# Attention scores on one core: operand rows copied by way of DRAM, row maxima carried as two fp32 halves, scores by key issued ahead of the wait for the maxima

## Chip, core and metric

One core of a Trainium2 chip runs the whole program. The metric is device time in microseconds of one execution. The kernel is written in raw instructions for five engines (TensorE, VectorE, ScalarE, GpSimd and SyncE; PE, DVE, ACT, POOL and SP in the rows), each with its own queue, and tied together with semaphores.

## What is computed

Four layers, each a cross attention and a feed-forward net, on 4096 tokens of 128 numbers (x) with a context of the same size. Three of the four attentions are the same kind and concern us: 16 heads of width 8, 32 tiles of 128 queries. The reference for them, cut to what matters:

```python
# L0: projections with biases
score = jnp.einsum('bhij,bhjk->bhik', qh, kt) / math.sqrt(d)      # d = 8
attn = jax.nn.softmax(score, axis=-1)
out = jnp.einsum('bhls,bhsd->bhld', attn, vh)
# L2: one set of keys and values shared by all 16 heads
attn_score = jnp.einsum('bhid,bjd->bhij', qh, k) / np.sqrt(D_HEAD)
# L3: as L0, with a mask by key and a causal mask
m = mask[:, None, :, None] + future[None, None, :, :]
scores = jnp.where(m != 0, NEG, scores)
```

A softmax needs the maximum of each row of scores. The kernel computes it exactly and takes it off before the exponential.

## The kernel before, in words

**Stages.** By the profile's clock the program runs: L0's attention (about 50 to 235 us), the feed-forward net, attention and net of the next layer (to 485), L2's attention (485 to 708), its net of eight experts (to 825), L3's attention (825 to 1090), and the last net (to 1162).

**A half.** An attention walks over 32 tiles, and each tile in two halves of 8 heads: 64 halves in an attention, 192 in all. The order on each engine is written out by hand, in `pair_of_scores(u, g, v, f)` and the functions around it. For one half TensorE does:

- *scores by key* for tile u into banks 2 and 3: keys on the partitions, 4 heads x 128 queries along a row. L1402 in L0, L1353 in L2 (one moving operand of 512 columns for each of two row groups), L1359 in L3 (8 instructions of 128 columns). They wait for t_ex, ScalarE having emptied banks 2 and 3.
- *scores by query* for tile v = u + 2 into banks 0 and 1, only to find the row maxima: L1405 in L0, L1362 in L2 and L3 (8 instructions of 128 columns). They wait for t_mx, VectorE having taken the maxima out of these banks (L1867), and for operands_in, the DMAs of their rows.
- In L3 both get a mask by further small bf16 matmuls ahead (L1390 by key, L1395 by query, 8 each).
- *the maxima*: L1416 adds minus the row maximum to banks 2 and 3, waiting for t_nm.
- ScalarE's exponential of the two banks (L1046, 128x1024), and on TensorE the weighted values of the half before (L1434, 8 instructions in two passes, 16 records).

The array's 128 rows are used as four groups of 32. The keys' scores of a half lie on two groups and the queries' scores on the other two, so instructions of both can run side by side. The maxima's matmul uses 12 rows of the same two groups as the keys' scores. The weighted values use all 128 rows.

**How a maximum reaches the banks.** VectorE reduces (L1867) to negative maxima, 16 numbers a query. They are split into three bf16 parts by four small operations: on GpSimd in L0 and L3 (`split_maxima`, L802 to L808), on VectorE in L2 (L1924, L1926, L1934, L1946). TensorE transposes the parts (L1485), and VectorE multiplies the transposed rows with 0/1 columns into `nmax_one` (L1904, 128x512 bf16), which L1416 sums over with ones as the stationary operand.

**Operand rows.** In L2 and L3 the projections are made per quad of four tiles (L1551, L1555, L1561), copied out by ScalarE (L1068 into `q_all`, L1078 into `k_all`), split by VectorE into upper bits and rest (L1875, L1878; t_half counts them). Then SP's `rows_of_quad` spreads them from SBUF to SBUF over the row groups (L599): 64 KB a DMA, 20 DMAs a quad in L2 (4 of k, 16 of q) and 32 in L3 (16 and 16). ScalarE may write `k_all` and `q_all` of the next quad only once all row DMAs of the quad before have landed (`staging_free`).

## Time and profile before

| | before |
|---|---|
| time, median of 3 runs | 1161.0 us (1151.83 to 1170.66) |
| the profiled execution | 1163.81 us, its span 1162.1 us |
| mean granted TensorE clock | 0.818 of full speed |
| busy: PE, DVE, ACT, POOL | 954.1, 772.6, 621.9, 471.6 us |
| chain that ended last | PE 59%, DVE 21%, issue 10%, ACT 3%, SP's queue 3% |

The page is one execution. "Busy" is the time an engine worked on instructions; "granted clock" is TensorE's clock in tenths or parts of full speed, which has the levels 1.0 (2.4 GHz) and 0.5 (1.2 GHz), so a mean of 0.75 over a stretch says that half of it was at each level. The chain is the sequence of work that ended last, and "issue" in it is time in which the engine waited for nothing that the profile shows.

### The profile page before, as it was taken

The numbers are of one execution on the slowest core, as the hardware profiler recorded it, in microseconds if no ns is written. First come the engines' busy times: TensorE is split into PE (matmuls) and PEld (weight loads), VectorE is DVE, ScalarE is ACT, GpSimd is POOL, SyncE is SP. The second block draws the span as 40 slices with busy tenths as digits, with TensorE's granted clock in tenths as the row PEclk, the third lists the DMA queues.
The fourth block names the chain that finished last, engine by engine and source line by source line (L and its number), as shares of the span: only waits on it lengthen the run. The fifth ranks groups of instructions, "written<-read, shape, count | busy, mean of one in ns | idle before, by whom it ended". The sixth has DMA issues, their size and how long they took to land.

```text
span 1162.1 us, 30498 instructions
## 1 busy us (share of the span) xinstructions
PE 954.1 (82%) x10213; PEld 661.9 (57%) x10213; DVE 772.6 (66%) x2053; ACT 621.9 (54%) x1387; POOL 471.6 (41%) x999
## 2 busy tenths in 40 slices
PE   3889898967777556789988899888698888899999
PEld 3644444424455233356666666787555556566798
DVE  3567877758978798488777764374258667765344
ACT  3556666547756566266455434455434455433366
POOL 5421467632145243102333445677411377773100
PEclk9999999975678687698667758999868888865699
DMA  6979676457799930222122205768442233330011
GB/s 181 157 82 90 63 99 81 69 114 173 95 177 181 176 54 1 56 75 54 51 56 55 56 11 158 200 170 262 118 117 74 75 93 110 111 92 2 3 34 36
DMA packets 326321, 112.33 MB, mean 97 GB/s; under 512 B 224873, under 2 KB 299657, under 8 KB 326186
## 3 DMA queue, kind: packets, MB, share of 16 engines
q1 hardware_dynamic: 319834, 94.40, 43.7%
q0 software_dynamic: 5488, 15.88, 4.4%
q8 instruction: 82, 1.34, 0.5%
q14 instruction: 53, 0.43, 0.1%
q10 hardware_dynamic: 864, 0.27, 0.1%
HBM read 50.70 MB, written 35.51 MB: 74 GB/s over the span
## 4 chain that ended last, share of the span: by engine, by line
PE 59%; DVE 21%; issue 10%; ACT 3%; SPq 3%; POOL 2%; DMA 2%; another core or an unknown queue 0%; DVEq 0%; ACTq 0%; POOLq 0%
PE bank L1434 8%; DVE nmax L1867 7%; PE bank L1402 5%; PE bank L1524 4%; PE bank L1416 3%; PE bank L1765 3%; PE bank L1719 3%; PE bank L1359 3%; PE bank L1731 3%; PE bank L1773 2%; SPq L599 2%; PE bank L1533 2%; PE bank L1362 2%; PE bank L1281 2%; PE bank L1561 2%
## 5 line engine op out<-in xcount | busy, mean ns | idle before, releaser
L1867 DVE TENSOR_REDUCE nmax<-bank 128x8 f32<-128x1024 f32 x192 | 234.5, 1221 | 126.6 <-PE bank L1362 83.9
L1046 ACT ACTIVATE probs_space<-bank 128x1024 f32<-128x1024 f32 x192 | 196.7, 1024 | 190.1 <-PE bank L1416 188.7
L1434 PE MATMUL bank<-probs_space,vals 128*32 128x128 f32 x3072 | 149.4, 322 | 3.0 <-issue 3.0
L1434 PEld LDWEIGHTS bank<-probs_space,vals 128*32 128x32 f32 x3072 | 84.9, 124 | 77.7 <-issue 70.5
L1362 PE MATMUL bank<-k_rows,q_rows 32*128 32x128 f32 x1024 | 106.7, 337 | 6.8 <-DMA q_rows<-q_all 6.8
L1362 PEld LDWEIGHTS bank<-k_rows,q_rows 32*128 32x128 f32 x1024 | 88.9, 241 | 10.0 <-DMA q_rows<-q_all 7.7
L802 POOL CAST nmax_parts<-nmax 128x16 bf16<-128x16 f32 x64 | 12.6, 198 | 198.8 <-DVE nmax L1867 184.7
L1416 PE MATMUL bank<-nmax_one,ones_bf 12*128 12x512 bf16 x384 | 91.0, 452 | 0.0
L727 POOL TENSOR_TENSOR var_b<-stats 128x8 f32<-128x8 f32 (+3 forms) x33 | 7.4, 225 | 203.3 <-DVE stats L1802 201.8
L1402 PE MATMUL bank<-q_one,k_all 32*128 32x512 f32 x256 | 72.9, 636 | 19.8 <-DVE nmax L1867 16.7
L1904 DVE TENSOR_TENSOR nmax_one<-bank,max_row 128x512 bf16<-128x512 bf16 x96 | 65.6, 684 | 20.2 <-PE bank L1485 17.0
L1405 PE MATMUL bank<-k_one,q_all 32*128 32x512 f32 x256 | 73.0, 643 | 1.7 <-DVE nmax L1867 0.9
L1802 DVE BATCH_NORM_STATS2 stats<-x 128x6 f32<-128x128 f32 x230 | 61.2, 287 | 5.0 <-DMA x<-in_x_dram 2.0
L960 POOL DMA_INDIRECT token_rows<-early,slot_row_int x46 | 48.6, 1057 | 30.0 <-DVE early L2245 21.2
L1931 DVE RECIPROCAL o_inv<-bank 128x16 f32<-128x16 f32 x96 | 24.4, 254 | 53.7 <-PE bank L1533 53.7
L786 POOL TENSOR_TENSOR late<-bf_up,late 128x512 f32<-128x512 f32 x36 | 56.7, 1598 | 0.1
L734 POOL TENSOR_TENSOR var_a<-var_b,minus_half 128x8 f32<-128x8 f32 (+3 forms) x33 | 53.9, 1633 | 2.6
L1731 PE MATMUL bank<-moe_w,probs_space 128*128 x368 | 50.4, 281 | 4.3 <-ACT probs_space L1241 2.3
L1353 PE MATMUL bank<-q_rows,k_rows 32*128 32x512 f32 x128 | 39.9, 614 | 16.7 <-DVE nmax L1867 15.5
L1359 PE MATMUL bank<-q_rows,k_rows 32*128 32x128 f32 x512 | 52.5, 331 | 0.0
L1731 PEld LDWEIGHTS bank<-moe_w,probs_space 128*128 128x128 f32 x368 | 46.0, 196 | 5.0 <-issue 5.0
L1266 ACT ACTIVATE q_one<-bank,up_bias 128x128 f32<-128x128 f32 x128 | 36.6, 369 | 20.4 <-PE bank L1765 20.4
(300 smaller groups left out, 2533.9 us busy)
## 6 DMA issues: line engine op xcount, KB each, us to landing
expert_rows<-zeros SPq DMA_DIRECT2D x8, 2322.0 KB, 34.6
q_rows<-q_all SPq DMA_DIRECT2D x256, 64.0 KB
k_rows<-k_all SPq DMA_DIRECT2D x160, 64.0 KB
context<-expert_w SPq DMA_DIRECT2D x31, 322.0 KB
k_one<-expert_w SPq DMA_DIRECT2D x15, 322.0 KB
late<-_L_ffn_down_weights_dram POOLq DMA_DIRECT2D x9, 512.0 KB, 5.6
late<-in_L_ffn_up_weights_dram POOLq DMA_DIRECT2D x9, 512.0 KB, 4.4
q_one<-expert_rows SPq DMA_DIRECT2D x46, 64.5 KB
```

The costliest lines, as they stand in the source:

```text
L786: pool.tensor_tensor(tmp(i), half(src, i % 2), weight, ALU.mult).then_inc(S("bf_step"), 1)
L1046: act.activation(probs[:, 2 * g:2 * g + 2, :, :].rearrange("k g i q -> k (g i q)"), bank_pair[1][:, :, :].rearrange("k g f -> k (g f)"), A ...
L1359: pe.matmul(bank[2 + s][:, at], operand(k_rows, u, 2 * g + s, i), operand(q_rows, u, 2 * g + s, i), start=not masked and i == 0, stop=False)
L1362: m = pe.matmul(bank[s][:, at], operand(q_rows, v, 2 * f + s, i), operand(k_rows, v, 2 * f + s, 0 if shared_keys else i), start=not masked ...
L1402: pe.matmul(bank[2 + s], group(k_all, u, 2 * g + s), group(q_one, u, 2 * g + s), start=True, stop=False)
L1405: m = pe.matmul(bank[s], group(q_all, v, 2 * f + s), group(k_one, v, 2 * f + s), start=True, stop=True)
L1416: m = pe.matmul(bank[2 + s], ones_bf[first:last, :], nmax_one[first:last, u % 2, :, :], start=False, stop=True)
L1434: m = pe.matmul(bank[4][32 * j:32 * j + 32, g * P:(g + 1) * P], v[:, first:first + VW], probs[:, 2 * g + j // 2, j % 2 * 2 + s, :], start= ...
L1731: m = pe.matmul(bank[(4, 6)[(t - 1) % 2]][:, 0:P], slot_hid[:, (t - 1) % 2, c * P:(c + 1) * P], w2[:, bass.ds(expert[t - 1] * HID + c * P, ...
L1802: dve.bn_stats(stats[:, u, :], x[:, u * P:(u + 1) * P]).then_inc(S("stats"), 1)
L1867: dve.tensor_reduce(nmax[:, u % 2, 0, :].rearrange("q (g i) -> q g i", i=HG)[:, 2 * g:2 * g + 2, :], bank_pair[0][:, :, :].rearrange("q g ...
L1904: dve.tensor_tensor(nmax_one[:, (t + 1) % 2, :, :], over_blocks(bank[6][:, 3 * P:4 * P].bitcast(BF16)[:, 0:P], HG), max_row[:, :].unsqueez ...
```

## The change

1. `NPART` is 2: a maximum is split into its upper bits and the rest, both fp32, by two small operations on VectorE in all three attentions (`halves_of_maxima`). GpSimd only waits for t_mx in its place.
2. VectorE's `nmax_one` goes. ScalarE copies the transposed 128x128 block to `nmax_rows` instead. The transposition is fp32.
3. The maxima's matmul: 8 instructions a half, each with a 0/1 column `max_row[rows, i]` broadcast over 128 columns as the stationary operand (8 rows) and 128 columns of `nmax_rows` moving, instead of 2 instructions of 12 rows and 512 columns.
4. The scores by key of a half, with their masks, are issued ahead of the waits for operands_in and t_mx and ahead of all scores by query. Before they were interleaved with them in L0 and L3.
5. Operand rows of q in L2, of q and k in L3: one DMA of the whole 512 KB tile to DRAM, a wait for it, and 4 DMAs of 256 KB back, one for each row group. 9 DMAs a quad in L2, 10 in L3. The first of a tile waits for both of its halves.

The core of the diff:

```diff
+            def rows_by_way_of_dram(halves, scratch, rows, of_row, out_name, n_out, name):
+                sp.dma_start(scratch[:, :, :], halves[:, :, :]).then_inc(S(out_name), 16)
+                sp.wait_ge(S(out_name), 16 * n_out)
+                for n in range(4):
+                    sp.dma_start(rows[n:P:4, :, :].bitcast(F32),
+                                 scratch[:, of_row[n], :].rearrange("(i r) f -> r i f", i=HG)).then_inc(S(name), 16)
...
                 def iteration(t):
+                    if live(t + 1):
+                        act.wait_ge(S("t_mt"), tiles + t + 2)
+                        past(act, "t_s2", 2 * (tiles + t))
+                        act.activation(nmax_rows[:, (t + 1) % 2, :], bank[6][:, 3 * P:4 * P], ACT.Copy
+                                       ).then_inc(S("t_nm"), 1)
...
                 def pair_of_scores(u, g, v, f):
                     if live(u):
+                        scores_by_key(u, g)
                     if live(v):
+                        scores_by_query(v, f)
...
                     if live(u):
                         pe.wait_ge(S("t_nm"), tiles + u + 1)
-                        for s in range(2):
-                            first = HR * (2 * g + s)
-                            last = first + NPART * HG
-                            m = pe.matmul(bank[2 + s], ones_bf[first:last, :], nmax_one[first:last, u % 2, :, :],
-                                          start=False, stop=True)
+                        for i in range(HG):
+                            for s in range(2):
+                                rows = slice(HR * (2 * g + s), HR * (2 * g + s) + NPART * HG)
+                                m = pe.matmul(bank[2 + s][:, i * P:(i + 1) * P],
+                                              max_row[rows, i:i + 1].broadcast_to([NPART * HG, P]),
+                                              nmax_rows[rows, u % 2, :], start=False, stop=i == HG - 1)
...
-                        dve.tensor_tensor(nmax_one[:, (t + 1) % 2, :, :], over_blocks(bank[6][:, 3 * P:4 * P].bitcast(BF16)[:, 0:P], HG),
-                                          max_row[:, :].unsqueeze(2).broadcast_to([P, HG, P]), ALU.mult
-                                          ).then_inc(S("t_nm"), 1)
...
+                        dve.tensor_scalar(upper.bitcast(I32), whole.bitcast(I32), UPPER_BITS, None, ALU.bitwise_and
+                                          ).then_inc(S("t_na"), 1)
...
+                        dve.tensor_tensor(rest, whole, upper, ALU.subtract).then_inc(S("t_na"), 1)
```

**TensorE in L2, one half, before.** L1353 are the scores by key, L1362 those by query, L1416 the maxima, L1434 the weighted values:

```order
L1485 MATMUL bank<-ident_bf,nmax_parts 128x128 [waits t_on,t_res,t_nm,t_na]
L1353 MATMUL bank<-q_rows_51,k_rows_55 128x512 [waits t_mx,operands_in1,t_ex]
L1353 MATMUL bank<-q_rows_51,k_rows_55 128x512
L1362 MATMUL bank<-k_rows_53,q_rows_49 128x128 x8
L1416 MATMUL bank<-nmax_one,ones_bf 128x512 [waits t_nm]
L1416 MATMUL bank<-nmax_one,ones_bf 128x512
L1434 MATMUL bank<-probs_space,vals 32x128 [waits t_ve,t_ue,t_ex]
```

The same place of the changed kernel (L1379 by key, L1398 by query, L1419 the maxima, L1438 the weighted values):

```order
L1489 MATMUL bank<-ident,nmax_halves 128x128 [waits t_on,t_res,t_nm,t_na]
L1379 MATMUL bank<-q_rows_51,k_rows_55 128x512 [waits t_ex]
L1379 MATMUL bank<-q_rows_51,k_rows_55 128x512
L1398 MATMUL bank<-k_rows_55,q_rows_51 128x128 [waits t_mx,operands_in0]
L1398 MATMUL bank<-k_rows_55,q_rows_51 128x128 x7
L1419 MATMUL bank<-nmax_rows,max_row 128x128 [waits t_nm]
L1419 MATMUL bank<-nmax_rows,max_row 128x128 x7
L1438 MATMUL bank<-probs_space,vals 32x128 [waits t_ve,t_ue,t_ex]
```

The waits for the maxima and for the rows moved from the first score by key to the first by query, and the maxima's matmul became eight instructions.

**TensorE in L3, one half, before** (L1390 and L1395 the masks by key and by query, L1359 and L1362 the scores by key and by query; a pair of each kind stands for eight):

```order
L1390 MATMUL bank<-quant_bf,future_rep 128x4x32 [waits t_mx,operands_in0,t_ex]
L1395 MATMUL bank<-ident_blocks_bf,past_rep 128x4x32
...
L1359 MATMUL bank<-q_rows_52,k_rows_56 128x128
L1362 MATMUL bank<-k_rows_53,q_rows_49 128x128
...
L1416 MATMUL bank<-nmax_one,ones_bf 128x512 [waits t_nm]
L1416 MATMUL bank<-nmax_one,ones_bf 128x512
L1434 MATMUL bank<-probs_space,vals 32x128 [waits t_ex]
```

The same place of the changed kernel (L1353 and L1376 mask and scores by key, L1362 and L1398 mask and scores by query):

```order
L1353 MATMUL bank<-ffn_wT,future_rep 128x4x32 [waits t_ex]
L1353 MATMUL bank<-ffn_wT,future_rep 128x4x32 x7
L1376 MATMUL bank<-q_rows_50,k_rows_54 128x128 x8
L1362 MATMUL bank<-ident_blocks_bf,past_rep 128x4x32 [waits t_mx,operands_in1]
L1362 MATMUL bank<-ident_blocks_bf,past_rep 128x4x32 x7
L1398 MATMUL bank<-k_rows_54,q_rows_50 128x128 x8
L1419 MATMUL bank<-nmax_rows,max_row 128x128 [waits t_nm]
L1438 MATMUL bank<-probs_space,vals 32x128 [waits t_ex]
```

Before, neighbours in the queue lie on different row groups and belong to different banks; now 16 instructions on two row groups stand ahead of 16 on the other two.

**SP in L3, the rows of a quad, before:**

```order
L599 DMA k_rows_53<-k_all 32x512 [waits t_half,t_s2]
L599 DMA k_rows_53<-k_all 32x512 x7
L599 DMA k_rows_53<-k_all 32x512 [waits t_half]
L599 DMA k_rows_53<-k_all 32x512 x7
L599 DMA q_rows_49<-q_all 32x512 [waits t_half]
L599 DMA q_rows_49<-q_all 32x512 x7
```

And changed:

```order
L606 DMA k_halves<-k_all 128x1024 [waits t_half,t_s2]
L609 DMA k_rows_53<-k_halves 32x4x512 [waits k_out]
L609 DMA k_rows_53<-k_halves 32x4x512 x3
L606 DMA q_halves<-q_all 128x1024 [waits t_half]
L609 DMA q_rows_49<-q_halves 32x4x512 [waits q_out]
L609 DMA q_rows_49<-q_halves 32x4x512 x3
```

Far fewer issues, and two waits for a DMA's completion that stand in SP's queue.

## Rows read from the trace of the kernel before

**Rows 1.** Windows: start:end, length, PE, PEld, DVE, ACT, POOL busy, clock, DMA.
```profile
75.00:225.00 150.00, 133.09 (x1574) 68.10 (x1570) 112.23 (x191) 98.32 (x160) 79.06 (x181) 0.99 0.71 83
490.00:705.00 215.00, 194.87 (x2160) 136.56 (x2158) 166.72 (x462) 108.86 (x200) 63.34 (x164) 0.71 0.19 49
845.00:1085.00 240.00, 212.60 (x3473) 144.70 (x3470) 155.44 (x275) 107.80 (x178) 115.52 (x225) 0.75 0.28 79
500.00:525.00 25.00, 20.74 (x327) 14.29 (x326) 22.36 (x50) 16.95 (x29) 0.00 (x0) 1.00 0.27 72
1050.00:1075.00 25.00, 25.00 (x342) 16.82 (x338) 13.44 (x23) 9.79 (x15) 8.92 (x23) 0.50 0.01 2
```

**Rows 2.** Timeline, L2 at full clock: start, duration, engine, line, output<-input, idle before.
```profile
512.17 0.68 DVE L1904 TENSOR_TENSOR nmax_one<-bank,max_row 128x512 bf16<-128x512 bf16 x1
512.40 0.50 PE L1353 MATMUL bank<-q_rows,k_rows 32*128 32x512 f32 x2 [1.15 <-DVE nmax L1867]
512.71 0.42 PE L1416 MATMUL bank<-nmax_one,ones_bf 12*128 12x512 bf16 x2
512.79 0.27 PE L1362 MATMUL bank<-k_rows,q_rows 32*128 32x128 f32 x2
513.06 0.64 PE L1434 MATMUL bank<-probs_space,vals 128*32 128x128 f32 x16
515.19 0.50 PE L1353 MATMUL bank<-q_rows,k_rows 32*128 32x512 f32 x2 [0.85 <-DVE nmax L1867]
```

**Rows 3.** Timeline, L2 at half clock, TensorE, same columns.
```profile
562.19 0.79 PE L1353 MATMUL bank<-q_rows,k_rows 32*128 32x512 f32 x2
562.79 0.65 PE L1416 MATMUL bank<-nmax_one,ones_bf 12*128 12x512 bf16 x2
562.90 0.41 PE L1362 MATMUL bank<-k_rows,q_rows 32*128 32x128 f32 x2
563.36 1.08 PE L1434 MATMUL bank<-probs_space,vals 128*32 128x128 f32 x16
565.10 0.79 PE L1353 MATMUL bank<-q_rows,k_rows 32*128 32x512 f32 x2
```

**Rows 4.** Timeline, L3 at full clock, TensorE.
```profile
907.80 0.21 PE L1390 MATMUL bank<-quant_bf,future_rep 32*128 32x128 bf16 x1 [1.04 <-DVE nmax L1867]
907.99 0.30 PE L1359 MATMUL bank<-q_rows,k_rows 32*128 32x128 f32 x1
908.47 0.41 PE L1416 MATMUL bank<-nmax_one,ones_bf 12*128 12x512 bf16 x2
```

**Rows 5.** Timeline, L3 at half clock, TensorE.
```profile
1056.22 0.28 PE L1390 MATMUL bank<-l_T,future_rep 32*128 32x128 bf16 x1
1056.58 0.45 PE L1359 MATMUL bank<-q_rows,k_rows 32*128 32x128 f32 x1
1057.48 0.65 PE L1416 MATMUL bank<-nmax_one,ones_bf 12*128 12x512 bf16 x2
```

**Rows 6.** One maxima part on VectorE: least/median/most ns, first and last start.
```profile
L1926 DVE TENSOR_TENSOR nmax<-nmax,nmax_parts x32: 174/175/309, 487.2 to 688.9; 128x16 f32<-128x16 f32 x32
```

**Rows 7.** ScalarE's copy of a transposed 128x128 block, same columns.
```profile
L1105 ACT ACTIVATE oT<-bank x96: 271/283/296, 91.1 to 1089.4; 128x128 f32<-128x128 f32 x96
```

**Rows 8.** Waits, 860 to 1090 us (L3): waiting instruction <- releaser: total, times, longest.
```profile
ACT k_all L1078 <- DMA q_rows<-q_all: 15.8, 5, 4.3
PE bank L1390 <- issue: 11.1, 5, 3.4
```

**Rows 9.** Timeline of SP's queue, ahead of L3.
```profile
818.25 10.94 SPq L599 DMA_DIRECT2D k_rows<-k_all  x16
829.23 10.17 SPq L599 DMA_DIRECT2D q_rows<-q_all  x16
```

**Rows 10.** DMA issues: count, KB each, median us from issue to landing.
```profile
x<-in_x_dram SPq DMA_DIRECT2D x2, 512.0 KB, 11.2
context<-token_rows SPq DMA_DIRECT2D x2, 512.0 KB, 5.0
```

More of the change, by code:

```diff
@@ L18 @@
 NG, HG = 4, 4
-NPART = 3
+NPART = 2
 HR = 32
@@ L214, in gated_layers, with halves_of_maxima @@
         ROW_BUFFERS = {"L2": (2, 0, 1), "L3": (0, 1, 3)}
+        def halves_of_maxima(v):
+            halves = nmax_halves[:, v % 2, :].rearrange("q (g n i) -> q g n i", g=NG, i=HG)
+            return nmax[:, v % 2, :].rearrange("q (g i) -> q g i", i=HG), halves[:, :, 0, :], halves[:, :, 1, :]
         def rows_of(buffers, layer, c):
@@ new lines, in mask_of_maxima @@
+                def mask_of_maxima(f):
+                    for b in range(HG):
+                        at = slice(HR * b, HR * b + HR)
+                        for s in range(2):
+                            rows = slice(HR * (2 * f + s), HR * (2 * f + s) + HR)
+                            pe.matmul(bank[s].rearrange("q (i k) -> q i k", i=HG)[:, :, at],
+                                      past_rep[rows, b, :], over_blocks(ident_blocks_bf[rows, :], HG),
+                                      start=b == 0, stop=False)
@@ new lines, in scores_by_key @@
+                def scores_by_key(u, g):
+                    if not own:
+                        pe.wait_ge(S("t_q23"), 2 * (u // QT + 1))
+                        pe.wait_ge(S("t_q01"), 2 * (u // QT + 1))
+                    past(pe, "t_ex", 2 * (tiles + u) + g)
+                    if masked:
+                        mask(u, g)
+                    for i in range(1 if layer != "L3" else HG):
+                        for s in range(2):
+                            if layer == "L3":
+                                pe.matmul(bank[2 + s][:, i * P:(i + 1) * P], operand(k_rows, u, 2 * g + s, i),
+                                          operand(q_rows, u, 2 * g + s, i), start=False, stop=False)
+                            elif own:
+                                pe.matmul(bank[2 + s], operand(k_rows, u, 2 * g + s, 0),
+                                          operand(q_rows, u, 2 * g + s, slice(0, HG)), start=True, stop=False)
+                            else:
+                                pe.matmul(bank[2 + s], group(k_all, u, 2 * g + s), group(q_one, u, 2 * g + s),
+                                          start=True, stop=False)
```

172 lines of the change are left out of this document (58 added, 114 removed).

## Prediction

> **What bounds the kernel now.** I read first the windows of the three attention stages, since the change touches nothing else. In L0, TensorE works 133.1 of 150 us at almost full clock, VectorE 112.2. In L2 it works 194.9 of 215 us at a mean clock of 0.71, in L3 212.6 of 240 us at 0.75 [rows 1]. A mean of 0.71 is 42% of the time at full clock and 58% at half, 0.75 is half and half. So the engine that sets the end changes with the clock, and I read one half of a tile at each level.
>
> L2 at full clock: from one first score to the next is 2.79 us (512.40 to 515.19), and before both TensorE had stood idle, for 1.15 and 0.85 us, until VectorE had the maxima [rows 2]. VectorE is busy 22.4 of 25 us there, TensorE 20.7 [rows 1]: VectorE is the bound, with 2.5 us of work a half. L2 at half clock: 2.91 us a half and no idle time before the next one [rows 3]; TensorE is the bound. L3 late in the stage: half clock, TensorE busy 25.0 of 25 us [rows 1]. L3 at full clock waits for VectorE as L2 does, 1.04 us in the half shown [rows 4]. Beside that L3 has a loss of its own: ScalarE's copy into k_all waits 15.8 us for the last row DMAs of the quad before, in 5 places, and TensorE's next mask loses 11.1 us behind it in 5 places [rows 8]. SP's queue needs 10.9 us for the 16 row DMAs of k of one quad and 10.2 for q's, which stand behind them [rows 9].
>
> **Maxima's matmul.** Now its start is 0.35 us ahead of the weighted values at full clock (512.71 to 513.06) and 0.57 us at half (562.79 to 563.36) [rows 2, 3]. It becomes four rounds of 128 columns on two row groups, in a 4-byte type. Four rounds of scores of that size take 0.48 us at full clock (907.99 to 908.47) and 0.90 us at half (1056.58 to 1057.48) [rows 4, 5]. If the rounds were all, the price would be 0.48 − 0.35 = 0.13 and 0.90 − 0.57 = 0.33 us a half; if a tail of some 0.13 us follows the last round, as it seems to do now, 0.26 and 0.46. I take 0.22 and 0.41. The second pass of the transposition lies within these bounds.
>
> **VectorE.** It loses the 0.68 us product once a tile [rows 2], 0.34 us a half. In L2 it also does two small operations instead of four, of 0.175 us each [rows 6]: another 0.17 us a half. In L0 and L3 it gains two of them, so its net relief is 0.17 us a half. GpSimd's relief is worth nothing, for its parts are ready a tile ahead. ScalarE takes on 0.28 us a tile [rows 7] and is busy 16.95 of 25 us in L2's full-clock stretch [rows 1], so it has the room. While its copy waits for the transposition, the next exponential is queued behind it, and that one needs the maxima anyway.
>
> **L0.** TensorE is the bound: 64 halves x 0.22 = +14 us. Its idle time is 16.9 of 150 us [rows 1], mostly waits for VectorE, 0.2 to 0.3 us a half; VectorE's relief of 0.17 takes back 11 of it. Sum +3 us, bounds −5 (all idle time gone by the early scores by key) and +14.
>
> **L2.** At full clock VectorE falls from 2.5 to 2.0 us a half and TensorE is late next, with 20.74/25 x 2.79 = 2.31, plus 0.22: 2.53, say 2.6 us instead of 2.79. At half clock TensorE gets 0.41 us longer. The 215 us are some 32 halves at full (90 us) and 32 at half clock (125 us, 3.9 us each with projections and routing). With the same share of clocks: 32 x −0.2 + 32 x 0.41 = +6 us. But the clock is half in stretches that follow idle time on TensorE (it is full through L0, where the idle share is 11%, and through the first 25 us shown of L2), and that idle time goes: 17% idle at full clock becomes some 3%. I assume that half of the slow halves turn fast: 48 x 2.6 + 16 x 4.3 = 194, −21 us. If all did, 64 x 2.6 = 166, −49 us.
>
> **L3.** Two waits go. The stall behind the row DMAs: a 512 KB write and four reads of 256 KB. Nearest rows: 5.0 us for 512 KB from DRAM, 11.2 us where the queues are crowded [rows 10]. Write and reads (together 512 KB again) take 10 us for k and as much for q, 20 us in all, against 21.1 now [rows 9], 45 if crowded. I read the 10 us as a bound from above, since the four reads are in flight beside each other and the queues are not crowded in L3 (DMA share 0.28 [rows 1]). I take 7 us each: the 11 us of issue [rows 8] go. The waits for the maxima are 27.4 idle us of 240 [rows 1] less these 11, so 16; the scores by key now run within them, and VectorE is faster. Against that 31 halves x 0.22 and 33 x 0.41 = +20. Sum with the same clocks: −11 − 16 + 20 = −7 us. With half of the slow halves turned fast, at 0.8 us each, −20 us. Bounds −35 and +5. This holds if scores by key and by query still lie beside each other, which is the first rival's point.
>
> **Stage starts.** L3's first 32 row DMAs take 21 us in SP's queue (818.25 to 839.4) [rows 9] with TensorE idle. With 7 to 10 us for k and as much for q the way by DRAM takes 14 to 20 us: −5 us, bounds −7 and 0; if the writes took the crowded 11.2 us, +11.
>
> The Trainium skill (DMA: Bandwidth & Descriptors, Anatomy of one DMA) puts a fixed cost of about 2 us on each DMA, most of it the receipt for the write. Two DMAs in a row, for k and then for q, would pay it four times, an estimate of 8 us; the stall and the start would still shorten, and no row here parts the fixed cost from the rest.
>
> **Sum.** +3 − 21 − 20 − 5 = −43 us. Against the profiled execution's 1163.8 us that is 1121; the execution lies 2.8 us above the median of 1161.0, so I forecast 1119 us.
>
> **Rival 1, slower: keys and queries one after the other.** In L3 16 instructions on two row groups now stand ahead of the 16 on the other two. Before they alternated, and four groups worked together: masks and scores of both took 0.67 us (907.80 to 908.47) or 1.26 us at half clock [rows 4, 5]. If TensorE starts no instruction ahead of an earlier one, the same work takes twice that. At half clock that is 1.26 us x 33 halves = +42 us. At full clock the waits cover 0.4 of 0.67: +9 us. The gain of the covered waits and of the clock goes with it: L3 = −11 + 20 + 51 = +60 us, in all 3 − 21 + 60 − 5 = +37, so 1200 us. For it speaks the order alone. Against it: a maxima's matmul at 512.71 starts before the last pair of scores by query at 512.79, which stands ahead of it in the queue and lies on other groups, and so at 562.79 and 562.90 [rows 2, 3]. So a later instruction passes an earlier one, at least over two. Over 16 nothing shows. It decides where the depth is under some 8 instructions. I give it 0.27.
>
> By the Trainium skill (TensorE: Matmul & The Clock Gate, Step-by-step) only weight loads are pulled ahead and matmuls stay in program order, which is this rival, 1200 us. The two pairs of rows named just now disagree with the strict form of it. The same passage gives the queue that looks ahead a depth of 64, within which these 32 instructions with their loads would fit if matmuls did pass.
>
> **Rival 2, no change: the clock stays as it is.** The longer maxima's matmul is paid where TensorE is the bound, and the shares of the clock don't move: +3 + 6 − 7 − 5 = −3, 1158 us. For it speaks that late L3 is at half clock while TensorE is busy all the time [rows 1], so a full queue alone doesn't bring the clock back. Chance 0.22.
>
> **The numbers.** The forecast has 0.51, with its own range of 1075 to 1145 (L2 −49, L3 −35 at one end, the smaller halves of each at the other). A measurement tells about 2% from no change, 23 us: faster is below 1138. Forecast's case: 0.46 faster, 0.05 same. Rival 2: 0.03 faster, 0.18 same, 0.01 slower. Rival 1: 0.01 same or faster, 0.26 slower. Faster 0.49, same 0.24, slower 0.27. The range of 1075 to 1205 leaves out less than 0.2.
>
> **What the changed profile would show.** The line L1419 about 0.5 us ahead of L1438 at full clock. In L2 VectorE's busy share falling from 89% to 75 or 80% at full clock, and TensorE's wait for L1867's successor mostly gone; a mean clock above 0.8 in L2 if the assumption on it is right, near 0.71 if rival 2 is. In L3 the first mask by query within 0.1 us of the first mask by key where both are released (rival 1: 0.6 us or more behind). No "issue" wait of several us at the masks, and k_all's copy without its wait. SP: 10 DMAs a quad within 15 us. I would be wrong most of all by the depth over which TensorE passes instructions, then by the clock.

## Result, and the profile after

The changed kernel takes 1139.0 us (median of 20 executions, 1121.2 to 1161.6) beside 1167.3 us of the kernel before (median of 20), 28.3 us or 2.4% less. Ratios with an interval, here and in the table of experiments, compare only the quicker executions of each kernel, those within some 1.5% of its quickest: 0.971, with a 95% interval of 0.967 to 0.974. The forecast was 1119 us against 1161.0, a ratio of 0.964. The numbers below are those of one profiled execution each (before 1163.8 us, after 1140.5 us).

The windows of the three attentions L0, L2 and L3, from the start of the first to the start of the last exponential of each: start:end, length, busy time of PE, PEld, DVE, ACT and POOL, granted clock, DMA share, GB/s.

```profile
64.30:256.60 192.30, 178.46 (x2242) 122.67 (x2243) 122.44 (x246) 119.27 (x215) 69.93 (x104) 0.96 0.63 73
507.50:700.40 192.90, 183.79 (x2470) 139.37 (x2472) 134.02 (x352) 110.85 (x228) 61.93 (x159) 0.80 0.22 72
852.80:1062.60 209.80, 201.14 (x3741) 157.36 (x3745) 150.08 (x297) 107.39 (x203) 89.73 (x97) 0.85 0.36 118
```

The same stretches of the kernel before, read in the same way from its trace, were 178.9, 204.5 and 225.7 us, at a clock of 0.99, 0.73 and 0.76. So L0 lost 13.4 us, L2 gained 11.6, L3 gained 15.9, and the stretch between L2 and L3 went from 157.5 to 152.4 us, −5.1. The rest of the span gave 4.1 us, together 23.3 (1162.1 to 1138.8). In all three attentions TensorE is now busy 93 to 96% of the time; its idle time fell from 19.7 to 9.1 us in L2 and from 27.4 to 8.7 us in L3.

Two of the costliest groups of the page. The first answers to VectorE's maxima of before (L1867), the second to the maxima's matmul L1416 (384 instructions, now 1536). VectorE's product (0.68 us each in [rows 2]) has no line any more.

```profile
L1872 DVE TENSOR_REDUCE nmax<-bank 128x8 f32<-128x1024 f32 x192 | 234.2, 1220 | 155.7 <-PE bank L1398 94.4
L1419 PE MATMUL bank<-nmax_rows,max_row 8*128 8x128 f32 x1536 | 154.0, 321 | 0.0
```

**How keys and queries lie beside each other.** TensorE's timeline in L3 at full clock, to be laid beside [rows 4]. L1353 and L1376 are mask and scores by key, L1362 and L1398 mask and scores by query, L1419 the maxima.

```profile
881.79 0.40 PE L1353 MATMUL bank<-quant_bf,future_rep 32*128 32x128 bf16 x8
881.99 0.30 PE L1376 MATMUL bank<-q_rows,k_rows 32*128 32x128 f32 x2
882.03 0.28 PE L1362 MATMUL bank<-ident_blocks_bf,past_rep 32*128 32x128 bf16 x4
882.14 0.27 PE L1376 MATMUL bank<-q_rows,k_rows 32*128 32x128 f32 x2
...
882.25 0.38 PE L1376 MATMUL bank<-q_rows,k_rows 32*128 32x128 f32 x4
...
882.47 0.27 PE L1419 MATMUL bank<-nmax_rows,max_row 8*128 8x128 f32 x2
882.49 0.27 PE L1398 MATMUL bank<-k_rows,q_rows 32*128 32x128 f32 x2
...
883.01 0.64 PE L1438 MATMUL bank<-probs_space,vals 128*32 128x128 f32 x16
```

The first mask by query starts at 882.03, when six of the eight scores by key that stand ahead of it in the queue have not started (882.14 and 882.25). It starts 0.24 us behind the first mask by key, neither at the same time nor behind all 16. The maxima then start at 882.47, ahead of the last scores by query. From the first mask to the weighted values is 1.22 us (881.79 to 883.01). Before it was 0.67 us to the maxima [rows 4] and 0.34 from there, 1.01.

At half clock, beside [rows 5]:

```profile
1039.96 0.61 PE L1353 MATMUL bank<-l_T,future_rep 32*128 32x128 bf16 x8
1040.33 0.46 PE L1376 MATMUL bank<-q_rows,k_rows 32*128 32x128 f32 x2
1040.37 0.50 PE L1362 MATMUL bank<-ident_blocks_bf,past_rep 32*128 32x128 bf16 x6
1040.58 0.42 PE L1376 MATMUL bank<-q_rows,k_rows 32*128 32x128 f32 x2
...
1041.22 0.42 PE L1419 MATMUL bank<-nmax_rows,max_row 8*128 8x128 f32 x2
...
1042.21 1.08 PE L1438 MATMUL bank<-probs_space,vals 128*32 128x128 f32 x16
```

2.25 us from the first mask to the weighted values, 1.26 + 0.58 = 1.84 before. 0.41 us more, which is the price of the maxima that the forecast took.

**L2 at full clock**, beside [rows 2]:

```profile
543.03 0.50 PE L1379 MATMUL bank<-q_rows,k_rows 32*128 32x512 f32 x2
543.13 0.44 PE L1398 MATMUL bank<-k_rows,q_rows 32*128 32x128 f32 x4
...
543.37 0.23 PE L1419 MATMUL bank<-nmax_rows,max_row 8*128 8x128 f32 x2
...
543.85 0.64 PE L1438 MATMUL bank<-probs_space,vals 128*32 128x128 f32 x16
...
545.19 0.50 PE L1379 MATMUL bank<-q_rows,k_rows 32*128 32x512 f32 x2
```

2.16 us a half (543.03 to 545.19) where it was 2.79, and these two halves start without the idle time of 1.15 and 0.85 us of before. Over the whole of L2 TensorE's wait for the maxima fell from 15.5 to 1.3 us, and it now waits 6.3 us for ScalarE's exponential at the scores by key. From the maxima to the weighted values 0.48 us instead of 0.35. VectorE's busy share at full clock is 87% in one stretch of 25 us (520 to 545) and 77% in another (507.5 to 535); it was 89%.

**SP's queue in L3**, the quickest quad, beside [rows 9]:

```profile
891.37 0.33 SPq L606 DMA_DIRECT2D k_halves<-k_all  x1
893.95 2.67 SPq L609 DMA_DIRECT2D k_rows<-k_halves  x4
897.15 0.33 SPq L606 DMA_DIRECT2D q_halves<-q_all  x1
901.50 2.53 SPq L609 DMA_DIRECT2D q_rows<-q_halves  x4
```

From the issue of a write of 512 KB to the first read behind it, which waits for the write, it is 2.58 and 4.35 us here, and all issues end 12.7 us after the first. Later in L3 the write of q takes up to 7.7 us (975.80 to 983.54), and the quads take 12.7 to 18.0 us. Before, the 32 issues of a quad took 21.1 us ahead of L3 and 21.6 to 23.8 us in it.

### The profile page after: what moved, and what is told of

Read it like the earlier page. It is cut to its first block, busy times and chain, and to the rows that moved or that the text cites. A ratio compares the mean times of both kernels' runs of the same rounds, so it can differ in the third digit from the quotient of the medians.

```text
span 1138.8 us, 32253 instructions
## 1 busy us (share of the span) xinstructions
PE 971.3 (85%) x11365; PEld 732.8 (64%) x11365; DVE 743.7 (65%) x2022; ACT 635.7 (56%) x1483; POOL 418.0 (37%) x743
## 4 chain that ended last, share of the span: by engine, by line
PE 57%; DVE 20%; issue 8%; ACT 6%; DMA 3%; POOL 3%; SPq 1%; another core or an unknown queue 0%; ACTq 0%; DVEq 0%; POOLq 0%
PE bank L1438 7%; PE bank L1419 5%; PE bank L1382 5%; DVE nmax L1872 5%; ACT probs_space L1042 4%; PE bank L1528 3%; PE bank L1398 3%; PE bank L1777 2%; PE bank L1769 2%; PE bank L1723 2%; PE bank L1735 2%; PE bank L1537 2%; PE bank L1379 2%; DVE small L2041 2%; DVE stats L1806 2%
## 5 line engine op out<-in xcount | busy, mean ns | idle before, releaser
L1419 PE MATMUL bank<-nmax_rows,max_row 8*128 8x128 f32 x1536 | 154.0, 321 | 0.0
L1419 PEld LDWEIGHTS bank<-nmax_rows,max_row 8*128 8x128 f32 x1536 | 128.8, 211 | 22.4 <-issue 18.1
L1438 PE MATMUL bank<-probs_space,vals 128*32 128x128 f32 x3072 | 141.7, 309 | 0.7 <-issue 0.7
L1398 PE MATMUL bank<-k_rows,q_rows 32*128 32x128 f32 x1024 | 96.5, 311 | 7.0 <-DMA q_rows<-q_halves 4.9
L1438 PEld LDWEIGHTS bank<-probs_space,vals 128*32 128x32 f32 x3072 | 81.2, 119 | 20.1 <-issue 4.2
L1398 PEld LDWEIGHTS bank<-k_rows,q_rows 32*128 32x128 f32 x1024 | 80.1, 216 | 11.8 <-issue 6.0
L1382 PE MATMUL bank<-q_one,k_all 32*128 32x512 f32 x256 | 75.7, 664 | 13.8 <-ACT probs_space L1042 13.4
L796 POOL TENSOR_TENSOR late<-bf_up,late 128x512 f32<-128x512 f32 x36 | 56.7, 1591 | 50.1 <-DVE nmax L1872 49.9
L956 POOL DMA_INDIRECT token_rows<-early,slot_row_int x46 | 48.6, 1057 | 35.0 <-DVE early L2232 26.2
L796 POOL TENSOR_TENSOR late<-bf_dn,late 128x256 f32<-128x256 f32 x36 | 31.3, 887 | 75.6 <-DVE nmax L1872 64.5
L1376 PE MATMUL bank<-q_rows,k_rows 32*128 32x128 f32 x512 | 45.9, 302 | 0.0
L941 POOL DMA_INDIRECT expert_rows<-late,dest_int x32 | 32.1, 1004 | 35.1 <-DVE dest_int L1963 28.1
```

The lines of the kernel that those rows point to most:

```text
L796: pool.tensor_tensor(tmp(i), half(src, i % 2), weight, ALU.mult).then_inc(S("bf_step"), 1)
L956: pool.indirect_dma_start(out=token_rows, out_offset=bass.IndirectOffsetOnAxis(ap=slot_row_int[:, s_no:s_no + 1], axis=0), in_=slot_y[:, s ...
L1382: pe.matmul(bank[2 + s], group(k_all, u, 2 * g + s), group(q_one, u, 2 * g + s), start=True, stop=False)
L1398: m = pe.matmul(bank[s][:, i * P:(i + 1) * P], operand(q_rows, v, 2 * f + s, i), operand(k_rows, v, 2 * f + s, 0 if layer == "L2" else i), ...
L1419: m = pe.matmul(bank[2 + s][:, i * P:(i + 1) * P], max_row[rows, i:i + 1].broadcast_to([NPART * HG, P]), nmax_rows[rows, u % 2, :], start= ...
L1438: m = pe.matmul(bank[4][32 * j:32 * j + 32, g * P:(g + 1) * P], v[:, first:first + VW], probs[:, 2 * g + j // 2, j % 2 * 2 + s, :], start= ...
```

## Experiments

The change has three parts that can stand alone: the maxima (M), the order (O) and the rows by way of DRAM (R). The kernels below have them one by one, in pairs and by layer. The theory was that of the forecast: each part pays or costs in its own place. The rival theory was that a part's worth depends on the others, since a wait taken away only shows the next one.

| kernel | parts | ratio to before | 95% | medians of all, us: this / before | L0, L2, L3: us from first to last exponential |
|---|---|---|---|---|---|
| before | | 1 | | | 178.9, 204.5, 225.7 |
| e3 | M | 1.013 | 1.004 to 1.022 | 1160.4 / 1153.2 | 193.7, 197.3, 225.3 |
| e8 | O | 1.006 | 1.001 to 1.011 | 1162.1 / 1162.5 | 179.1, 203.2, 226.2 |
| e7 | R | 0.975 | 0.968 to 0.981 | 1131.0 / 1162.5 | 179.0, 201.9, 201.9 |
| e6 | O, R | 0.970 | 0.962 to 0.977 | 1128.5 / 1162.5 | 176.2, 204.8, 201.6 |
| e1 | M, R | 0.997 | 0.990 to 1.004 | 1146.4 / 1153.2 | 208.9, 195.1, 225.3 |
| e2 | M, O | 1.004 | 0.998 to 1.011 | 1153.9 / 1153.2 | 193.1, 178.1, 230.0 |
| after | M, O, R | 0.971 | 0.967 to 0.974 | 1139.0 / 1167.3 | 192.2, 192.9, 209.7 |
| e5, the same again | M, O, R | 0.972 | 0.960 to 0.984 | 1139.0 / 1162.5 | 198.2, 198.0, 210.0 |
| e4 | O, R; M not in L0 | 0.966 | 0.955 to 0.977 | 1102.2 / 1153.2 | 178.4, 168.3, 209.9 |
| e9 | O, R; M in L2 alone | 0.959 | 0.949 to 0.969 | 1121.5 / 1165.2 | 178.3, 192.9, 199.2 |
| e10 | R; M in L2 alone | 0.970 | 0.964 to 0.977 | 1132.3 / 1165.2 | 183.6, 208.0, 200.1 |
| e11 | R in L3 alone | 0.975 | 0.969 to 0.981 | 1134.8 / 1165.2 | 178.9, 205.5, 200.4 |
| e12 | R, each tile written 3 times | 1.056 | 1.049 to 1.062 | 1230.3 / 1165.2 | 177.6, 217.5, 270.3 |

The last column is one execution each, and L2's length in it moves with the granted clock. In executions of one and the same kernel the time follows the clock too: of the changed kernel's 20, the one at a mean clock of 0.822 took 1161.6 us and one at 0.864 took 1121.2 us. e1's profile is the slowest of its executions, at 0.809. Each kernel is compared with executions of the kernel before on the same chip, which themselves have medians from 1153.2 to 1167.3 us. So the ratios decide, and the last column only where differences are large or come back in several kernels.

Read as a cube of three parts, the ratios say: R is worth 1.6 to 3.6% in all four of its pairs (before to e7, e8 to e6, e3 to e1, e2 to after). M costs 1.3% alone (e3) and 2.2% beside R (e7 to e1), and nothing clear of the noise beside O (e8 to e2, e6 to after). O gives 2.6% beside M and R (e1 to after); beside M (0.9%) and beside R (0.5%) the intervals overlap, and alone it is 0.6% slower.

**e1: order of before, maxima and rows as changed.** In `pair_of_scores`:

```diff
-                    if live(u):
-                        scores_by_key(u, g)
-                    if live(v):
-                        scores_by_query(v, f)
...
+                    if live(u):
...
+                        past(pe, "t_ex", 2 * (tiles + u) + g)
+                    if live(v):
+                        if own:
+                            name, landed = operands_in(layer, v // QT)
+                            pe.wait_ge(S(name), landed)
...
+                        past(pe, "t_mx", 2 * (tiles + v) + (1 - f))
...
+                    if own:
+                        scores_of_heads(u, g, v, f)
```

> The changed kernel with the matmuls' order and waits of before: the wait for the maxima and the rows stands ahead of the first score by key, and in L0 and L3 scores by key and by query alternate again. Theory A (the early scores by key fill waits for the maxima in L3 and L2): L3's attention, 209.7 us from first to last exponential, goes up by 8 to 16 us, L2's (192.9) by 2 to 5, L0's (192.2) stays; in all some 1152 us. Theory B (the early issue is worth nothing, and 16 instructions on two row groups ahead of the other 16 delay the scores by query by the 0.4 us that the trace shows at half clock): L3 goes down by 5 to 10 us, in all 1132 us.

Ratio 0.997 where the whole change has 0.971: taking the order back costs some 2.6%, about 30 us, more than twice what theory A had. Theory B falls. By stages L3 rose by 15.6 us and L2 by 2.2, as A had it, but L0 rose by 16.7 us too, where A had nothing; its clock was 0.88 beside 0.96. This one profile is of the slowest execution, so how the loss divides over the stages is not shown. In L3 TensorE again waits 11.9 us for the maxima, 4.0 in the changed kernel.

**e2: row DMAs of before, maxima and order as changed.**

```diff
-        N_ROW_DMAS = {"L2": 4 + 4, "L3": 4 + 4}
+        N_ROW_DMAS = {"L2": HG * (1 + HG), "L3": HG * (HG + HG)}
...
-                    rows_by_way_of_dram(k_all, k_halves, rows_of(k_rows, layer, c), K_HALVES, "k_out", c + 1, name)
+                                    sp.dma_start(rows_of(buffers, layer, c)[n:P:4, i, :].bitcast(F32),
+                                                 halves[HR * at:HR * at + HR, upper, :]).then_inc(S(name), 16)
```

> The changed kernel with the row DMAs of before (20 a quad in L2, 32 in L3, from SBUF to SBUF). Theory A (the way by DRAM took away ScalarE's stall ahead of k_all and shortened the idle stretch before L3): L3 goes up by about 11 us, the stretch from L2's last to L3's first exponential (152.4 us) by 5, in all 1155 us. Theory B (the stall was only the place where TensorE's slack showed): less than 3 us more in L3, in all 1144 us.

Ratio 1.004: without the rows nothing of the gain is left, 3.3% or nearly 40 us, more than theory A's 16 us. The two profiled executions are 18.7 us apart: L3 rose by 20.3 us (A had 11), the stretch ahead of it by 5.8, and L2 fell by 14.8 us at a clock of 0.88 beside 0.80. The waits in L3 (850 to 1080 us; waiting instruction, releaser, total, times, longest):

```profile
ACT k_all L1070 <- DMA q_rows<-q_all: 9.5, 4, 4.1
PE bank L1358 <- DMA q_rows<-q_all: 6.3, 3, 3.4
```

TensorE no longer stands before the masks for the maxima; it stands before those by query (L1358), for the rows. The early scores by key uncovered the late rows.

**e3: the maxima alone** (the changed kernel with the two edits of e1 and e2 together).

> The kernel of before with the new maxima alone (two fp32 halves on VectorE, ScalarE's copy, eight matmuls of 8 rows): old order, old row DMAs. Theory A (each part acts in its own stage): L0 up by 13 us as in the changed kernel (178.9 to 192), L2 down by 8 to 12 (204.5 to 194), L3 up or down by under 5: 1165 to 1170 us beside 1167 of before. Theory B (VectorE's relief is only worth something once the early scores by key are there): L2 stays at 204 us and the kernel is 10 to 20 us slower than before, 1180 us.

Ratio 1.013, and 1.006 by the medians. L0 at 193.7 us, +14.8, L2 at 197.3, −7, L3 the same: theory A nearly stage by stage. Its total, within 3 us of before, is missed: 7 us slower by the medians, 15 by the ratio, whose interval ends above 1. A half in L3 at half clock in the old order shows the price of the maxima's matmul alone:

```profile
1056.66 1.06 PE L1413 MATMUL bank<-nmax_rows,max_row 8*128 8x128 f32 x8
1057.65 1.08 PE L1432 MATMUL bank<-probs_space,vals 128*32 128x128 f32 x16
```

0.99 us from its start to the weighted values, 0.57 before in L2 [rows 3]: +0.42.

**e4: the maxima of before in L0 alone.**

```diff
+                            if layer == "L0":
+                                m = pe.matmul(bank[2 + s], ones_bf[first:first + 3 * HG, :],
+                                              nmax_one[first:first + 3 * HG, u % 2, :, :], start=False, stop=True)
...
+                    if live(t + 1) and layer == "L0":
+                        dve.tensor_tensor(nmax_one[:, (t + 1) % 2, :, :], over_blocks(bank[6][:, 3 * P:4 * P].bitcast(BF16)[:, 0:P], HG),
+                                          max_col[:, :].unsqueeze(2).broadcast_to([P, HG, P]), ALU.mult
+                                          ).then_inc(S("t_nm"), 1)
```

> The changed kernel, but L0 keeps the maxima of before (three bf16 parts by GpSimd, VectorE's product, two matmuls of 12 rows and 512 columns); L2 and L3 are as changed, order and rows too. Theory A (L0's +13 us is the longer maxima's matmul, 64 x 0.2 us, on an engine that has no slack there): L0 falls from 192 back to about 179 us, in all 1126 us, faster than both kernels. Theory B (L0 lost the time by the order, all scores by key ahead of the wait): L0 stays at 190 us or more, in all 1138 us.

L0 is back at 178.4 us with the new order in it: theory A. The order did not cost L0 its time; the maxima did. TensorE is busy 163.4 us in this L0 and 178.5 in the changed kernel's, a difference of 15.0 us, about that of the lengths (13.8). The edit puts back the split, the product and the matmul of two instructions at once, so it doesn't say which of them it is. The ratio of 0.966 is below the change's, though the intervals overlap.

**e5: the changed kernel once more**, on the same chip as e6 to e8.

> The changed kernel once more, on the same chip as the next three, as their measure. Both theories: 2 to 3.5% under the kernel of before (0.965 to 0.98).

0.972, as before.

**e6: order and rows without the new maxima.**

```diff
-NPART = 2
+NPART = 3
...
-                        for i in range(HG):
-                            for s in range(2):
-                                rows = slice(HR * (2 * g + s), HR * (2 * g + s) + NPART * HG)
...
+                        for s in range(2):
...
+                            m = pe.matmul(bank[2 + s], ones_bf[first:last, :], nmax_one[first:last, u % 2, :, :],
+                                          start=False, stop=True)
```

> The kernel of before with the new order and the way by DRAM, the maxima as before (the third part of the change left out). Theory A (each part pays in its own place, and the new maxima cost L0 13 us and give L2 some 10): L0 at 179 us from first to last exponential, L2 at 195 to 203, L3 at 205 to 212; 20 to 30 us faster than before, as fast as the whole change. Theory B (the early scores by key and the faster rows only pay once VectorE is relieved): L3 stays above 218 us and the kernel within 10 us of before.

0.970, L3 at 201.6 us: theory A, and more than it said in L3; L2, at 204.8, gained nothing. The whole change, with the new maxima, has 210 us in L3: there they cost 8 us.

**e7: the rows alone**, the kernel of before with the new `rows_of_quad`.

> The kernel of before with the way by DRAM alone. Theory A (the two losses seen in the trace of before go: 11 us of issue behind ScalarE's k_all, 5 us of start): 12 to 18 us faster than before, L3 at 212 to 216 us, no wait of k_all's copy for a DMA. Theory B (taking the rows away from the kernel with the early scores cost 29 us by the medians, so rows are worth most where the rest is fast): under 10 us faster here.

0.975. One part, nearly all of the whole change's gain. L3 falls from 225.7 to 201.9 us, 24 us where theory A had 10 to 14. One wait of k_all's copy for the rows is left, 3.8 us.

Where in L3 the time went is seen when the stage is cut in two: from the 1st to the 49th of its 64 exponentials (six quads), and from there to the last (two quads). The columns are those of the windows above. First the kernel before:

```profile
857.89:1026.92 169.03, 141.63 (x2626) 97.20 (x2629) 122.81 (x222) 82.07 (x140) 87.79 (x172) 0.85 0.34 95
1026.92:1083.60 56.68, 56.68 (x741) 39.32 (x745) 26.87 (x47) 21.19 (x33) 26.06 (x46) 0.50 0.10 28
```

e7:

```profile
849.10:1012.32 163.22, 138.78 (x2626) 96.16 (x2629) 126.93 (x222) 81.75 (x139) 88.19 (x172) 0.86 0.42 136
1012.32:1051.04 38.72, 35.55 (x741) 25.56 (x744) 26.23 (x47) 19.52 (x33) 26.39 (x46) 0.91 0.15 51
```

The changed kernel:

```profile
852.84:1005.39 152.55, 145.59 (x2916) 113.02 (x2917) 123.08 (x242) 85.58 (x163) 68.92 (x76) 0.93 0.46 148
1005.39:1062.57 57.18, 55.47 (x831) 44.28 (x830) 26.95 (x56) 21.78 (x40) 20.81 (x22) 0.64 0.11 38
```

And e6:

```profile
857.60:1021.09 163.49, 148.95 (x2629) 112.75 (x2632) 129.16 (x221) 81.56 (x139) 88.00 (x171) 0.84 0.41 136
1021.09:1059.19 38.10, 35.82 (x741) 27.46 (x738) 26.48 (x48) 19.51 (x33) 26.56 (x47) 0.91 0.14 48
```

Before and e7 do the same work. TensorE's idle time is the same too, 27.4 and 27.6 us. 5.8 of the 24 us were saved in the first 48 halves, where the stalls were, and 18.0 in the last 16, which took 56.7 us at half clock before and 38.7 at 0.91. Before, TensorE works 1.87 of the 4 us from 1022 to 1026, then the clock falls and stays at half to the end of the stage, though TensorE is busy without a gap. In e7 it falls at about 1013, is back at full at about 1019 and stays there. So most of the gain is the same instructions run faster at the end of the stage. What decides whether the clock comes back is not shown.

The other kernels repeat this within a few microseconds. With the new rows and the old maxima in L3 (e6, e7, e9, e10, e11) the last 16 take 38.1 to 38.7 us; in all others 53.6 us or more. With M, O and R in L3 (after, e5, e4) the two parts are 152.6 to 152.8 and 57.2 us. So the 8 us that the new maxima cost L3 beside O and R are a gain of 11 us in the first part and a loss of 19 in the second, where the changed kernel's clock falls for the last time at 1028 and does not rise again.

**e8: the order alone.**

> The kernel of before with the new order alone. Theory A (scores by key run in the wait for the maxima, 16 us in L3 and 15 us in L2): 8 to 15 us faster than before, TensorE's wait for VectorE's maxima under 6 us in L3. Theory B (the wait only moves: VectorE is the bound at full clock, the row DMAs come next): within 5 us of before, and TensorE waits for the row DMAs at the scores by query.

1.006, and 1.000 by the medians: no gain. Theory B, by these waits in L3 (850 to 1080 us):

```profile
ACT k_all L1078 <- DMA q_rows<-q_all: 22.0, 5, 6.8
PE bank L1361 <- DMA q_rows<-q_all: 15.6, 6, 5.1
PE bank L1361 <- DVE nmax L1869: 2.0, 4, 0.7
```

TensorE's wait for the maxima, 16.2 us before, is 2.0 us; 15.6 us of wait for the rows have come instead, and ScalarE's wait for them grew from 15.8 [rows 8] to 22.0.

**e9 and e10: new maxima in L2 alone, with the new and with the old order.** e9 is e4 with L3 treated as L0; e10 has e1's edit besides.

```diff
-                            if layer == "L0":
+                            if layer != "L2":
```

> The changed kernel with the new maxima in L2 alone: L0 and L3 keep three bf16 parts by GpSimd, VectorE's product and two matmuls of 12 rows and 512 columns; new order and rows everywhere. Theory A (the new maxima's matmul costs where TensorE is the bound, 0.2 us a half at full and 0.4 at half clock, and pays only in L2, where VectorE is): L0 177 to 180 us from first to last exponential, L2 168 to 195 by the clock granted, L3 200 to 203 instead of 210; a ratio of 0.945 to 0.96. Theory B (L3's 210 us with the new maxima beside 202 without were the difference of two executions): L3 stays at 208 or more and the ratio at 0.965.

> The same with the order and waits of before. Theory A (the early scores by key are worth nothing by themselves, as the order alone showed: 1.006): within 0.5% of the kernel above. Theory B (they pay where the row DMAs are fast and VectorE is relieved, as taking the order back from the whole change cost 1.4 to 2.5%): 10 to 20 us slower than the kernel above, most of it in L2.

e9 has the lowest ratio of all, 0.959: L0 178.3, L3 199.2, as theory A had it. Its interval ends at 0.969, below the change's estimate of 0.971 but not clear of its interval. By the medians of all executions e4 is ahead (0.956 beside 0.963), so which of the two is faster is not settled. e10 has 0.970; the order is worth 1% here, 11 us by the medians, and in the profiles 15 us in L2 (208.0 to 192.9) and 5 in L0. That is theory B of e10, with overlapping intervals. The order's worth beside the new maxima has the same sign in three pairs (e1 to after, e3 to e2, e10 to e9), and only the first is clear of the noise; without them it is no gain (before to e8) or half a percent within the noise (e7 to e6).

**e11: the way by DRAM in L3 alone.**

```diff
+                if layer == "L3":
+                    rows_by_way_of_dram(k_all, k_halves, rows_of(k_rows, layer, c), K_HALVES, "k_out", c + 1, name)
```

> The kernel of before with the way by DRAM in L3 alone (L2 keeps its 20 DMAs a quad). Theory A (ScalarE's stall was L3's: 32 issues a quad; L2's 20 fit): L3 at 202 us as with both, L2 at 202 to 205, ratio 0.975 to 0.98. Theory B: L2 gives a part too, and the ratio is 0.985 or more.

0.975, L3 at 200.4 and L2 at 205.5 us: the same as in both layers. With the old maxima L2's 20 DMAs a quad were in time anyway. With the new ones they are not quite: in L2 ScalarE's copy into k_all waits 7.9 us for them in e3 and 9.5 in e2.

**e12: each whole tile written three times.**

```diff
+                for again in (1, 2, 3):
+                    sp.dma_start(scratch[:, :, :], halves[:, :, :]).then_inc(S(out_name), 16)
+                    sp.wait_ge(S(out_name), 48 * (n_out - 1) + 16 * again)
```

> The kernel of before with the way by DRAM, each whole tile written to DRAM three times in a row, each time waited for, ahead of the four reads: some 6 us more for k and as much for q in a quad. Theory A (with 10 DMAs the rows have slack of over 10 us a quad, and being in time is all that they need): L3 at 202 to 206 us, only the stretch ahead of L3 longer by some 8 us; ratio 0.98. Theory B (every us in which the rows are later moves the work behind them): L3 at 212 to 226 us, k_all's copy waits for a DMA again, ratio 0.995 to 1.0.

1.056, much worse than theory B's 1.0. SP's queue for a quad:

```profile
908.04 7.18 SPq L604 DMA_DIRECT2D k_halves<-k_all  x3
917.50 2.53 SPq L607 DMA_DIRECT2D k_rows<-k_halves  x4
920.08 8.40 SPq L604 DMA_DIRECT2D q_halves<-q_all  x3
931.71 2.52 SPq L607 DMA_DIRECT2D q_rows<-q_halves  x4
```

and the waits in L3 (870 to 1150 us):

```profile
ACT k_all L1086 <- DMA q_rows<-q_halves: 52.4, 6, 10.4
PE bank L1398 <- issue: 47.0, 6, 9.7
```

The rows take 26.2 us from the first issue to the end of the last (908.04 to 934.23), 2 to 5 more than before, and L3 grows to 270.3 us, 45 more than before. ScalarE may write k_all only when q's last row of the quad before has landed, and ScalarE's next exponential is queued behind that copy. So a late row stops a ring of four engines, and the quads follow each other at the pace of the rows: 35.2 us from one to the next (908.04 to 943.22). With the old maxima L3 orders by the rows' issues a quad: 13 to 17 us give 199 to 202 us (e6, e7, e9, e10, e11), 21 to 24 give 226 (before, e8), 25 to 27 give 270 (e12). The new maxima break this order: e1 has 12 to 16 us a quad and an L3 of 225.3.

## Why the prediction was right or wrong

The direction came true, and the time lies within the forecast's own range of 1075 to 1145 us. The size is about half: −43 us were forecast, and the profiled executions are 23.3 us apart, the medians 28.3. L0 fell short by 10.4 us, L2 by 9.4, L3 by 4.1, and 4.1 us came from stretches that the sum left out. Two steps held, the price of the matmul and the start of L3. (The sum itself gives 1118, 1163.8 − 43 − 2.8; the 1119 is a slip of 1 us.) Of the signs, k_all's copy still waits 3.0 us for the rows in L3, and SP's 10 DMAs take 12.7 to 18.0 us a quad where 15 was the limit.

**Price of the maxima's matmul: right.** 0.22 and 0.41 us a half were taken; the traces show 0.13 us more from its start to the weighted values in L2 at full clock, 0.21 more in L3 from the first mask on, and 0.41 or 0.42 at half clock (after, e3).

**L0, +3: wrong, it was +13.4 (e3: +14.8, e5: +19).** The sum was 14 for the matmul less 11 for VectorE's relief. TensorE's busy time in L0 rose by 19.1 us (159.35 to 178.46), and its idle time fell by 5.7 (19.6 to 13.8). Two steps failed. The first is that L0 stays at full clock. Cut into eighths of 8 exponentials each, six of them are at full clock in the changed kernel and cost 4.4 us together, near the forecast. The third and the sixth are not, and cost 8.9. These two before:

```profile
107.29:131.68 24.39, 21.00 (x248) 11.13 (x248) 19.45 (x34) 15.32 (x26) 8.04 (x22) 1.00 0.63 48
178.56:201.36 22.80, 20.48 (x244) 10.65 (x244) 16.98 (x30) 15.26 (x26) 16.52 (x35) 1.00 0.79 94
```

and after:

```profile
110.38:136.95 26.57, 24.20 (x296) 16.86 (x296) 18.07 (x38) 15.98 (x31) 5.34 (x7) 0.94 0.56 44
185.82:215.36 29.54, 28.00 (x292) 18.33 (x292) 16.69 (x34) 16.22 (x30) 13.28 (x19) 0.77 0.60 72
```

L0 was at a clock of 0.88 to 0.96 in the kernels with the new maxima in it, and at 0.95 to 1.00 in the others. Why it falls there is not shown. The second failed step is "VectorE's relief of 0.17 takes back 11 of it". TensorE's wait for the maxima did vanish. In its place stands a wait of nearly the same length, in the changed kernel's L0 (64 to 257 us):

```profile
PE bank L1382 <- ACT probs_space L1042: 13.4, 22, 2.3
DVE nmax L1872 <- PE bank L1402: 55.5, 39, 3.2
```

The scores by key now wait for ScalarE's exponential in 22 places, as they waited for the maxima in 22 places before, 16.5 us then. The exponential is behind the maxima's matmul, so its added time is on this ring too; that is argued from the order, and no run parts it. VectorE has more idle time than before. e4 shows that it is the maxima: with the old ones L0 is at 178.4 us.

**L2, −21: half of it, −11.6.** The period at full clock fell further than forecast (2.16 us in the half shown, 2.6 taken). But the assumption that half of the slow halves turn fast came out at the clock going from 0.73 to 0.80, which is 54% of the time at half clock falling to 40%, a quarter of them. In five executions of kernels with new maxima and new order L2 took 168.3, 178.1, 192.9, 192.9 and 198.0 us at clocks of 0.92, 0.88, 0.80, 0.79 and 0.76. They differ in where the clock first falls: in e4 the first six eighths of L2 are at full clock (19.1 to 21.1 us each), in the changed kernel the first four. So the size of this term is the clock's, and one execution doesn't fix it; −6 to −36 us are all seen. Kernels with the old maxima had 202 to 206 us (before, e6, e7, e8, e11), those with the new ones and the old order 195.1, 197.3 and 208.0 (e1, e3, e10). So the new maxima shorten L2 in most executions, and more with the new order; that it needs both is not shown.

**L3, −20: near by its sum (−15.9), by luck, for its parts are wrong.** Forecast were −11 for the stall, −16 for the waits for the maxima, +20 for the matmul, and −13 for the clock. Measured: the rows alone give −24 (e7, e11), the new maxima cost 8 (e6 and e9 against after and e5), and the order gives nothing without them (e8: 226.2; e6 against e7: 201.6 and 201.9). The step that failed is to price the rows by the stall that the trace shows. Of their 24 us only 6 lie where the stalls were, and 18 in the last 16 halves, which before ran at half clock throughout.

**Stage start, −5: right, though not by the −5.1 above.** That stretch was 159.1 us with the new rows in e6 and 151.0 with the old ones in e3, so it doesn't measure the term. From the first row DMA to L3's first exponential it does: 39.6 and 39.4 us (before, e8) became 33.7 in e7 and e6, −6. k and q took 10.9 and 10.2 us of issues ahead of L3 [rows 9]; in the changed kernel the two writes with their waits and four reads each make some 13 us. The Trainium skill (DMA: Bandwidth & Descriptors, Anatomy of one DMA) has about 2 us of fixed cost a DMA, on the path of DMAs that GpSimd issues. The ones here are SyncE's; a write of 512 KB with its completion in 2.58 us leaves room for little more than that.

**Rival 1 (keys and queries one after the other, 1200 us): did not come.** The masks by query start when four to six of the scores by key ahead of them are still to start. The marker of the forecast, "within 0.1 us", was too strict: it is 0.24 us at full and 0.41 us at half clock. It costs nothing on the way to the weighted values: e6 has 1.04 us from the first mask to them at full clock, before it was 1.01:

```profile
1039.52 0.40 PE L1359 MATMUL bank<-l_T,future_rep 32*128 32x128 bf16 x8
...
1040.20 0.39 PE L1425 MATMUL bank<-nmax_one,ones_bf 12*128 12x512 bf16 x2
...
1040.56 0.64 PE L1443 MATMUL bank<-probs_space,vals 128*32 128x128 f32 x16
```

The Trainium skill (TensorE: Matmul & The Clock Gate, Step-by-step) says that the matmuls themselves stay in program order. These traces disagree for the starts of matmuls on different row groups (882.03 against 882.14 and 882.25).

**Rival 2 (the clock stays, 1158 us): did not come in L3** (0.76 to 0.85) and came by half in L2.

What stays open: why the clock of L2 differs so much from one execution to the next of the same kernel, while L3's repeats; what lets it come back in L3's last 16 halves; in which stages the new order pays beside the new maxima, since e1's single profile puts 16 us of it in L3 and 17 in L0. Also untested is which part of the new maxima costs (the split, ScalarE's copy, the fp32 transposition or the eight matmuls), and, of the rows, whether it matters that they pass through DRAM or only that SP has fewer DMAs to issue; e12 shows only that their time matters.

## What to carry to other kernels

When a change has several parts, price each by building it alone and beside the others: here one part out of three (10 DMAs by way of DRAM instead of 32 small ones in one queue) carried nearly the whole gain, one cost time in two stages out of three, and one was worth something only beside another. A transfer ring that is only just in time, 21 to 24 us of issues a quad, hides the worth of everything else: the order alone turned 16 us of one wait into 16 us of another. And a stall's worth can't be read from its length. With the rows' stall gone the idle time was the same, and three quarters of the gain came later in the stage, from the clock: look at the granted clock part by part, not at its mean.

## What the runs showed of the hardware

TensorE starts a matmul ahead of earlier ones in its queue that lie on other row groups: six scores by key had not started when the first mask by query did (882.03 against 882.14 and 882.25; at half clock 1040.37 against 1040.58), and four in the half at 884.61. None of the masks by query started with more than six scores still ahead of it in the halves shown. What sets this depth is not shown.

TensorE can be busy without a gap and stay at half clock: 56.7 us of L3's end before (1026.92 to 1083.60), at 0.50 throughout. The same 16 halves took 38.7 us in e7.

Eight fp32 matmuls of 8 rows and 128 columns, two at a time on two row groups, take 0.48 us at full clock and 0.99 us at half to the start of the next work. Two bf16 ones of 12 rows and 512 columns take 0.35 and 0.57 [rows 2, 3].

A 64 KB DMA from SBUF to SBUF costs its queue 0.65 to 0.75 us to issue (32 in 21.1 us [rows 9], 23.8 at most in L3), one of 256 KB from DRAM the same (4 in 2.5 us), and one of 512 KB to DRAM is complete after 2.6 to 7.7 us.
